# A four-layer graph network on one core: sums of three layers by scans, and row buffers released in quarters

## The chip, the cores and the metric

The kernel runs on 1 core of one Trainium2 chip, as a single program. The metric is the device time of one execution in microseconds (us), lower is better. Each row of a profile below is of one profiled execution. Engines: PE is TensorE, DVE is VectorE, ACT is ScalarE, POOL is GpSimd (it issues the gathers here), SP is SyncE (it issues the other loads and stores).

## What is computed

A graph has 6250 nodes with 64 features and 106250 edges (50000 pairs in both directions and a self-loop per node), sorted by destination. Four layers follow one another; each adds its result to x and normalizes:

```python
x = _layernorm(x + _L0_gnn_ref(x, L0_gnn_weight, src, dst, edge_type_16))        # sum over edges of x[src] @ W[type], 16 types
x = _layernorm(x + _L1_gnn_ref(x, L1_gnn_beta, src, dst))                        # softmax over a node's edges of the cosine of both ends
x = _layernorm(x + _L2_gnn_ref(x, edge_index, W_l, W_r, att, bias))              # GATv2 attention with 6 heads of 64
x = _layernorm(x + _L3_gnn_ref(x, W, coeff, h_bias, loop_weight, src, dst, edge_type_8))   # 2 bases, 8 types, plus x @ loop_weight
```

In each layer the core of the work is the same: a row of features per edge is fetched by the edge's source, weighted, and summed over the edges of one destination (`segment_sum`). The edges are in order of destination, so such a sum is a running sum that begins anew where the destination changes.

## The kernel before, in words

**Layout.** Edges lie over 128 partitions in NC = 832 columns; each partition holds a run of consecutive edges. Work goes in chunks of CH = 16 columns, NCH = 52 of them. `gf` holds one number per edge: 1 where the edge has the destination of the edge before it, 0 where a new one begins. The layers come one after another, and each has its loop over the 52 chunks.

**Gathers.** For each column POOL issues one indirect DMA that fetches 128 rows of a table in DRAM by the edges' sources (`gather`, L189, its instruction at L190), 16 per chunk. They go into a ring of buffers, and before a chunk's first gather POOL waits until the chunk that had the buffer is done with: in layer 0 (`linear_chunk_g`, L491, ring of N0 = 8) until the sums of it and of the first column after it are formed and stored; in layer 1 (`g1_chunk`, ring of 4) until the product of rows and weights (L838, L839) is made; in layer 2 (`g2_chunk`, L1165, ring of NX = 5) until all products of that chunk are made, DVE's (semaphore p2) and the 33 of ACT (semaphore ap, L1366 and L1371); in layer 3 (`basis_chunk_g`, L1640, ring of 4) until the product (L1663) is made. Layer 0's first FR = 5 chunks are made from the raw input and stand outside the change.

**Running sums.** DVE forms them column by column: SCALAR_TENSOR_TENSOR computes this column = previous column x gf + this column, on 64 (layer 0, L514), 65 (layer 1, L850), 390 (layer 2, L1385) or 128 elements (layer 3, L1673) per partition. Each instruction raises a semaphore and each waits for the one before it, as its input is that one's output. Layer 1 also spreads the destination's own row over its edges that way (`fill1`, L779, into PSUM; layer 2 does it at L1191). SP stores each chunk's sums in DRAM (s0 to s3). When a layer's last chunk is stored, POOL gathers the sum at each node's last edge from there ("s<-AR" is the store; "AR<-s,endi" the gather of ends), which starts the work per node.

**Beside the sums in layer 0** DVE prepares something else for the next layers. For 26 of its chunks two histograms run per chunk: DVE writes one-hots (L364, L366), PE multiplies them (L372, 16 small matmuls per histogram), and the next one-hots wait for that (semaphore hpe). After each chunk's histograms come two small operations of `twin_v` (L2052, L2055), then the 16 accumulations: `for c in range(FR, NCH): hists, twins, linear_chunk_v`.

**Layer 1** interleaves by hand, on DVE: the sums of chunk c (`step1`), the nine softmax steps of chunk c+1 (`soft1`, L800 to L820), the fill of c+2 (`fill1`); ACT makes the exponentials of c+1 (`exp1_a`, L828, L829) and DVE the product (`px1`, L838, L839).

**Layer 2** uses all engines: PE transposes the rows (L1205), multiplies with the weights (L1220, out by ACT at L1227), forms the logits with 32-column weights (L1236, out by ACT at L1244), and transposes these (L1251, out by ACT at L1256); DVE makes the softmax; products of weights and rows are made for some heads by DVE (L1354) and for two heads per column by ACT (L1371, `px2_a`); DVE sums (L1385).

**Layer 3**: a one-hot of the edge type (L1650), its product with the coefficients (L1652) and a reduction (L1655) give two weights per edge; L1663 multiplies rows and weights (2048 elements), then the 16 accumulations (L1673). In chunks 8 to 14 the self-loop's products are added: `turn3_a` (ACT copies a transposed block out of PSUM), PE at L1705, DVE at L1715 and L1717 (`loop3_v`). In ACT's queue the seven `turn3_a` stand right behind layer 2's work, with nothing else between.

## Time and profile before

| | us |
|---|---|
| median of 3 runs | 6202.34 (6194.47 to 6212.94) |
| the profiled execution | 6149.63 |
| its span, first to last instruction | 6147.8 |
| PE busy | 1595.5 |
| DVE busy | 2871.9 |
| ACT busy | 1115.1 |
| POOL busy | 3520.1 |

The profiled execution lies 52.7 us under the median. A busy time is the sum of an engine's instructions, register and semaphore work not counted. "Waits" of an engine are its idle time, by what ended it. In such lines "remote" stands where the profile shows no instruction that ended right then. The chain that ended last goes 39% through DVE and 3% through POOL.

### The profile page before, as it was taken

Reading aid. Unit: us, or ns where it says so; the run is one execution under the profiler, and the core shown is the slowest. Engines: PE = TensorE matmul, PEld = TensorE weight load, DVE = VectorE, ACT = ScalarE, POOL = GpSimd, SP = SyncE. Lnnn points to the kernel's source line nnn. Section 1 sums busy time; section 2 is a strip of 40 time slices with the busy share of each in tenths; the row PEclk is TensorE's granted clock in tenths of the full one; section 3 lists DMA queues with packets and bytes.
Section 4 is the critical chain, followed back from the end, with each engine's and each line's share of the span. In section 5 each row is a group of like instructions: output and inputs, shape, how many; then the busy total and the mean of one; then the engine's idle time right before and its main releaser. Section 6 shows DMA issues by size and latency. Waiting matters only on the chain.

```text
span 6147.8 us, 31588 instructions
## 1 busy us (share of the span) xinstructions
PE 1595.5 (26%) x6543; PEld 813.1 (13%) x6543; DVE 2871.9 (47%) x7562; ACT 1115.1 (18%) x3419; POOL 3520.1 (57%) x3636
## 2 busy tenths in 40 slices
PE   5531110000000000002375566666664500000002
PEld 1421110000000000001122222222221400000001
DVE  2344444125354455544255565555556632444344
ACT  1100000000000000001155555555555400000000
POOL 5355666766666666664634544454442576676754
PEclk7765555555555555556687888888887655555555
DMA  4212222221222222221123333333334221222222
GB/s 140 105 53 62 65 67 72 72 67 61 51 72 65 64 70 72 69 67 37 49 103 122 140 139 129 125 140 139 129 124 157 67 67 54 65 79 76 67 68 72
DMA packets 185944, 529.62 MB, mean 86 GB/s; under 512 B 70454, under 2 KB 75170, under 8 KB 169480
## 3 DMA queue, kind: packets, MB, share of 16 engines
q1 hardware_dynamic: 65816, 395.51, 17.0%
q0 software_dynamic: 117696, 129.81, 10.5%
q10 hardware_dynamic: 2224, 2.13, 0.1%
q14 instruction: 151, 1.24, 0.1%
q8 instruction: 57, 0.93, 0.1%
HBM read 185.57 MB, written 341.44 MB: 86 GB/s over the span
## 4 chain that ended last, share of the span: by engine, by line
DVE 39%; another core or an unknown queue 24%; issue 18%; PE 11%; ACT 5%; POOL 3%; DMA 1%; DVEq 0%; ACTq 0%; POOLq 0%; SPq 0%
DVE AR L1673 10%; DVE AR L514 5%; DVE ps L779 5%; PE ps L1220 4%; POOL AR L190 2%; PE ps L1236 2%; DVE AR L850 2%; DVE AR L1385 2%; ACT AR L1371 2%; DVE AR L364 1%; DVE AR L1663 1%; ACT AR L1227 1%; DVE AR L800 1%; PE ps L680 1%
## 5 line engine op out<-in xcount | busy, mean ns | idle before, releaser
L190 POOL DMA_INDIRECT AR<-xt,Si x2496 | 2402.0, 962 | 1687.3 <-issue 743.9
L190 POOL DMA_INDIRECT AR<-y,R x752 | 721.4, 959 | 520.9 <-issue 222.2
L1385 DVE SCALAR_TENSOR_TENSOR AR<-AR,gf 128x390 f32<-128x390 f32 x780 | 484.2, 621 | 654.3 <-ACT AR L1371 458.3
L1220 PE MATMUL ps<-AR,WLR 128*128 128x512 f32 x1248 | 681.7, 673 | 131.6 <-ACT AR L1227 88.2
L1673 DVE SCALAR_TENSOR_TENSOR AR<-AR,gf 128x128 f32<-128x128 f32 x831 | 295.0, 355 | 472.6 <-DVE AR L1673 360.1
L1371 ACT ACTIVATE AR<-AR 128x64 f32<-128x64 f32 x1664 | 495.5, 346 | 0.0
L1227 ACT ACTIVATE AR<-ps 128x512 f32<-128x512 f32 x624 | 368.5, 591 | 210.9 <-remote 146.7
L779 DVE SCALAR_TENSOR_TENSOR ps<-ps,gf,AR 128x64 f32<-128x64 f32 x831 | 242.2, 291 | 303.5 <-remote 160.5
L514 DVE SCALAR_TENSOR_TENSOR AR<-AR,gf 128x64 f32<-128x64 f32 x831 | 237.5, 286 | 258.2 <-DVE AR L514 155.5
L190 POOL DMA_INDIRECT AR<-s,endi x196 | 215.5, 1100 | 186.8 <-issue 112.4
L1220 PEld LDWEIGHTS ps<-AR,WLR 128*128 128x128 f32 x1248 | 238.8, 216 | 436.7 <-issue 312.5
L1354 DVE TENSOR_TENSOR AR<-AR,ps 128x512 f32<-128x512 f32 x416 | 282.8, 680 | 5.3 <-ACT ps L1329 5.3
L850 DVE SCALAR_TENSOR_TENSOR AR<-AR,gf 128x65 f32<-128x65 f32 x780 | 217.4, 279 | 100.7 <-remote 64.2
L1191 DVE SCALAR_TENSOR_TENSOR AR<-AR,gf 128x64 f32<-128x64 f32 x831 | 229.8, 277 | 48.4 <-DVE AR L1191 23.5
L364 DVE TENSOR_TENSOR AR<-AR,ps 128x1568 bf16<-128x1568 int32 x52 | 92.7, 1783 | 315.9 <-remote 291.4
L828 ACT ACTIVATE ps<-AR 128x17 f32<-128x17 f32 (+1 forms) x52 | 9.8, 188 | 1250.9 <-remote 431.8
L372 PE MATMUL ps<-AR 128*98 128x64 bf16 x832 | 80.1, 270 | 560.8 <-DVE AR L366 433.8
L1743 PE MATMUL ps<-ident,AR 128*128 128x128 f32 x1 | 0.5, 477 | 809.4 <-DVE AR L1673 809.4
L1992 ACT ACTIVATE AR<-AR 128x7 f32<-128x7 f32 x7 | 1.5, 208 | 1114.0 <-DVE AR L633 1067.9
L1236 PE MATMUL ps<-AR,A 128*32 128x512 f32 x1248 | 203.5, 604 | 0.0
L1016 PE MATMUL ps<-AR,ones 128*128 128x384 f32 (+1 forms) x6 | 3.7, 758 | 708.3 <-DVE AR L967 708.3
L1251 PE MATMUL ps<-ident,AR 128*128 128x128 f32 x208 | 55.3, 417 | 492.2 <-issue 319.1
(324 smaller groups left out, 2987.6 us busy)
## 6 DMA issues: line engine op xcount, KB each, us to landing
s<-AR SPq DMA_DIRECT2D x51, 3168.0 KB
AR<-xd SPq DMA_DIRECT2D x104, 512.0 KB
s<-AR SPq DMA_DIRECT2D x51, 1024.0 KB
AR<-xt,Si POOLq DMA_INDIRECT x2496
s<-AR SPq DMA_DIRECT2D x53, 512.0 KB
s<-AR SPq DMA_DIRECT2D x51, 528.0 KB
xd<-AR SPq DMA_DIRECT2D x52, 512.0 KB
y<-AR SPq DMA_DIRECT2D x24, 1024.0 KB
```

The source lines that it names most:

```text
L190: g.indirect_dma_start(out=o, out_offset=None, in_=table, in_offset=bass.IndirectOffsetOnAxis(ap=idx, axis=0)).then_inc(S[sem], 16)
L514: v.scalar_tensor_tensor(out=buf[:, j, :], in0=buf[:, j - 1, :] if j else prev[:, CH - 1, :], scalar=gf[:, c * CH + j:c * CH + j + 1], in1 ...
L779: v.scalar_tensor_tensor(out=xf1(c, j), in0=xf1(c, j - 1) if j else xf1(c - 1, CH - 1), scalar=gf[:, c * CH + j:c * CH + j + 1], in1=XBv[: ...
L850: v.scalar_tensor_tensor(out=Sv[:, j, 0:65], in0=Sv[:, j - 1, 0:65] if j else Sp[:, CH - 1, 0:65], scalar=gf[:, c * CH + j:c * CH + j + 1] ...
L1191: v.scalar_tensor_tensor(out=cur[:, j, D:P], in0=cur[:, j - 1, D:P] if j else prv[:, CH - 1, D:P], scalar=gf[:, c * CH + j:c * CH + j + 1] ...
L1220: t.matmul(PS[2 + k % 3][:], WLR[:, ch * P:(ch + 1) * P], XT2[:, u % 6, :], start=True, stop=True).then_inc(S["pm"], 1)
L1227: s.activation(RL2[:, u % 5, ch * 512:(ch + 1) * 512], PS[2 + k % 3][:], ACT.Relu).then_inc(S["ar"], 1)
L1236: m = t.matmul(PS[6][32 * q:32 * q + 32, :], w_, m_, start=(ch == 0), stop=(ch == 3))
L1354: v.tensor_tensor(s2v(c)[:, cols, 0:n * 65].rearrange("p j (h d) -> p j h d", h=n)[:, :, :, 0:D], bc(xsv(c)[:, cols, 0:D].unsqueeze(2), [P ...
L1371: s.activation(Sv[:, j, h * 65:h * 65 + D], xsv(c)[:, j, 0:D], ACT.Copy, scale=pe_[:, h, j:j + 1]).then_inc(S["ap"], 1)
L1385: m = v.scalar_tensor_tensor(out=Sv[:, j, 0:HW], in0=Sv[:, j - 1, 0:HW], scalar=gf[:, c * CH + j:c * CH + j + 1], in1=Sv[:, j, 0:HW], op0= ...
L1673: v.scalar_tensor_tensor(out=cur[:, j, :], in0=cur[:, j - 1, :] if j else prv[:, CH - 1, :], scalar=gf[:, c * CH + j:c * CH + j + 1], in1= ...
```

## The change

**Layers 0 (from chunk 5), 1 and 3.** The chain of 16 accumulations is replaced by scans. A `tensor_tensor_scan` computes, element after element along a partition, state = gate x state + data, here over 512 elements at a time. For this the data have to lie with the column as the fastest index, (d, j) in place of (j, d), and the gate has to be there for every element. So per chunk:

- ACT fills a PSUM bank with the gates (`gates_a`, 480 elements; the elements of column 0 stay at the 0 to which DVE's memset set the bank once: 4 banks ahead of layer 0's loop, 3 in layer 1, 3 + 1 in layer 3);
- in layer 0 ACT copies the gathered rows into a transposed tile (`turned0_a`), in layer 1 the destination's rows (`turned1_a`); the products of layers 1 and 3 are written transposed by DVE;
- DVE adds the previous chunk's last column in one instruction (semaphore st), then scans (semaphore sc): 2 of 512 elements in layer 0; 2 of 512 for the fill and 2 of 512 and one of 16 for the sums in layer 1; 4 of 512 in layer 3;
- ACT copies the sums out in store order (`summed0_a`, `summed1_a`, `summed3_a`: 1024, 1040, 2048 elements; semaphore co), and SP stores when co is raised, not when DVE is done.

POOL's releases: layer 0 now waits for the store alone (it ran that wait before too); layer 1 as before; layer 3 still for the product (m3). Layer 1's loads of destination rows wait for ACT's copy (cx).

**Order.** Layer 0's loop on DVE is now carry, twins, scans, then the two histograms. In layer 3 the three small weight operations of the next chunk stand between product, carry and scans of this one. The seven `turn3_a` now stand in ACT's queue in the middle of layer 3's loop (chunks 6 to 12), ahead of that chunk's copy out. Layer 1's last chunk is stored in halves instead of quarters, and the small `ends_v` of layer 1 moves from chunk 20 to chunk 49.

**Layer 2.** Its sums stay as they were. POOL's wait for the row buffer, once ahead of 16 gathers, becomes four waits, one ahead of each 4 gathers, for the products of the matching 4 columns.

```diff
@@ layer 0 @@
+        def gates_a(bank, at, n):
+            return s.copy(bank[:].rearrange("p (d j) -> p d j", j=n)[:, :, 1:n],
+                          bc(gf[:, at + 1:at + n].unsqueeze(1), [P, 512 // n, n - 1]))
...
+        def turned0_a(e, i):
+            c, j0, n = UN0[i]
+            e.wait_ge(S["late" if j0 else f"g_{c % N0}"], 16 * n if j0 else 16 * CH * (c // N0) + 16 * n)
+            if i >= 2:
+                e.wait_ge(S["st"], i)
+            s.copy(t0v(i), ring0(c)[:, j0:j0 + n, :].rearrange("p j d -> p d j")).then_inc(S["cx"], 1)
+
+        def summed0_a(e, i):
+            c, j0, n = UN0[i]
+            e.wait_ge(S["sc"], scans_upto(UN0, D, i + 1))
+            s.copy(ring0(c)[:, j0:j0 + n, :], t0v(i).rearrange("p d j -> p j d")).then_inc(S["co"], 1)
...
+            v.scalar_tensor_tensor(out=t0v(i)[:, :, 0], in0=row, scalar=gf[:, c * CH + j0:c * CH + j0 + 1],
+                                   in1=t0v(i)[:, :, 0], op0=ALU.mult, op1=ALU.add).then_inc(S["st"], 1)
...
+            for k in range(n * D // 512):
+                part = TT0[:, i % 2, k * 512:(k + 1) * 512]
+                v.tensor_tensor_scan(part, gx0(i)[:], part, 0.0, ALU.mult, ALU.add).then_inc(S["sc"], 1)
...
             if c >= N0:
                 e.wait_ge(S[f"s_{b}"], 16 * (c // N0))
-                e.wait_ge(S["lin0"], lin_at(c - N0 + 1, 0))
...
             for c in range(FR, NCH):
+                carry0_v(e, c - FR)
+                twin_v(e, 2 * (c - FR))
+                twin_v(e, 2 * (c - FR) + 1)
+                scan0_v(e, c - FR)
                 for h in hists(c):
                     hist_v(e, vc, 0, h)
-                twin_v(e, 2 * (c - FR))
-                twin_v(e, 2 * (c - FR) + 1)
...
-                linear_chunk_v(e, c)
@@ layer 1 @@
             for c in range(NCH):
-                exp1_a(e, c)
+                if c + 2 < NCH:
+                    gates1_a(e, c + 2)
+                    turned1_a(e, c + 2)
+                if c + 1 < NCH:
+                    exp1_a(e, c + 1)
+                summed1_a(e, c)
@@ layer 2 @@
         def g2_chunk(e, c):
-            if c >= NX:
-                e.wait_ge(S["p2"], p2_end(c - NX))
-                e.wait_ge(S["ap"], 33 * (c - NX + 1))
             for j in range(CH):
+                if c >= NX and j % 4 == 0:
+                    e.wait_ge(S["p2"], p2_end(c - NX) - 6 + j // 2)
+                    e.wait_ge(S["ap"], 33 * (c - NX) + 1 + 2 * (j + 4))
                 gather(xsv(c)[:, j, 0:D], xt2, Si[:, c * CH + j:c * CH + j + 1], f"g_{2 * (c % NX) + j // 8}")
@@ layer 3, on DVE, i a chunk or half of the last @@
+            v.tensor_tensor(sum3(i).rearrange("p (b d) j -> p j b d", b=NBS), bc(rows.unsqueeze(2), [P, n, NBS, D]),
+                            bc(CW3[:, i % 2, :, 0:n].rearrange("p b j -> p j b").unsqueeze(3), [P, n, NBS, D]),
+                            ALU.mult).then_inc(S["m3"], 1)
+            if more:
+                weight3_v(e, i + 1, 0)
...
+            for k in range(n * W3 // 512):
+                part = SUM3[:, i % 2, k * 512:(k + 1) * 512]
+                v.tensor_tensor_scan(part, gx3(i)[:], part, 0.0, ALU.mult, ALU.add).then_inc(S["sc"], 1)
+                if more and k == 0:
+                    weight3_v(e, i + 1, 2)
@@ layer 3, ACT's queue @@
-            for q in range(NG):
-                turn3_a(e, q)
+            gates3_a(e, 0)
+            for i, (c, j0, n) in enumerate(UN3):
+                if 6 <= c < 6 + NG:
+                    turn3_a(e, c - 6)
+                if i + 1 < len(UN3):
+                    gates3_a(e, i + 1)
+                summed3_a(e, i)
```

## Rows read from the trace of the kernel before

**Rows 1.** The page: busy time of each engine over the whole span.

```profile
PE 1595.5 (26%) x6543; PEld 813.1 (13%) x6543; DVE 2871.9 (47%) x7562; ACT 1115.1 (18%) x3419; POOL 3520.1 (57%) x3636
```

**Rows 2.** Busy time by stage; columns in the first line.

```profile
core 0: us, PE busy (x) PEld busy (x) DVE busy (x) ACT busy (x) POOL busy (x), PEclk, DMA share, GB/s
417.20:1041.60 624.40, 77.04 (x800) 70.42 (x800) 296.11 (x579) 0.00 (x0) 378.16 (x401) 0.50 0.22 63
1041.60:1351.00 309.40, 1.20 (x4) 1.00 (x4) 75.91 (x270) 0.00 (x0) 236.42 (x240) 0.50 0.26 77
1351.00:1406.60 55.60, 2.33 (x3) 1.17 (x4) 31.87 (x107) 0.00 (x0) 0.02 (x1) 0.50 0.31 124
1543.00:2764.20 1221.20, 1.46 (x4) 1.00 (x4) 594.78 (x2131) 16.23 (x100) 787.70 (x833) 0.50 0.26 67
2764.20:2804.20 40.00, 0.79 (x2) 0.50 (x2) 33.07 (x117) 0.65 (x4) 0.00 (x0) 0.50 0.14 55
2972.00:4631.50 1659.50, 1010.46 (x3763) 419.77 (x3756) 898.22 (x2300) 847.45 (x2602) 817.84 (x833) 0.81 0.36 125
4867.00:6030.20 1163.20, 30.19 (x122) 25.89 (x122) 450.71 (x1000) 3.85 (x13) 796.96 (x832) 0.50 0.23 67
6030.20:6064.70 34.50, 1.16 (x3) 0.68 (x3) 27.56 (x62) 0.27 (x1) 0.00 (x1) 0.50 0.26 104
```

**Rows 3.** POOL's longest waits for a buffer, layers 0 to 3: us, times, longest.

```profile
POOL AR L190 <- DVE AR L514: 140.2, 16, 15.1
...
POOL AR L190 <- DVE AR L839: 181.1, 16, 18.3
...
POOL AR L190 <- ACT AR L1371: 596.6, 47, 51.7
...
POOL AR L190 <- DVE AR L1663: 115.4, 15, 21.2
```

**Rows 4.** Timeline of layer 0 with histograms: start, duration, operation, [idle before].

```profile
584.76 1.54 PE L372 MATMUL ps<-AR 128*98 128x64 bf16 x16 [7.42 <-issue]
...
602.97 0.94 POOL L190 DMA_INDIRECT AR<-y,R  x1 [0.30 <-issue]
608.74 1.79 DVE L364 TENSOR_TENSOR AR<-AR,ps 128x1568 bf16<-128x1568 int32 x1 [24.04 <-remote]
...
613.73 0.94 POOL L190 DMA_INDIRECT AR<-y,R  x1 [9.81 <-DVE AR L514]
```

**Rows 5.** Timeline of layer 3, DVE, at two places.

```profile
5242.17 6.16 DVE L1673 SCALAR_TENSOR_TENSOR AR<-AR,gf 128x128 f32<-128x128 f32 x16
...
5690.99 2.29 DVE L1663 TENSOR_TENSOR AR<-AR,ps 128x2048 f32<-128x2048 f32 x1 [1.07 <-DVE ps L1655]
...
5702.79 0.35 DVE L1673 SCALAR_TENSOR_TENSOR AR<-AR,gf 128x128 f32<-128x128 f32 x1 [1.00 <-DVE AR L1673]
...
5718.99 2.29 DVE L1663 TENSOR_TENSOR AR<-AR,ps 128x2048 f32<-128x2048 f32 x1 [1.07 <-issue]
```

**Rows 6.** Timeline of layer 1, DVE's product of three chunks in a row.

```profile
1632.36 1.21 DVE L838 TENSOR_TENSOR AR<-AR,ps 128x1024 f32<-128x1024 f32 x1
...
1680.05 1.21 DVE L838 TENSOR_TENSOR AR<-AR,ps 128x1024 f32<-128x1024 f32 x1
...
1691.56 1.21 DVE L838 TENSOR_TENSOR AR<-AR,ps 128x1024 f32<-128x1024 f32 x1
```

**Rows 7.** Timeline of layer 2: PE's last logits, ACT's copy, POOL's next gather.

```profile
4389.65 1.04 PE L1236 MATMUL ps<-AR,Vm 128*32 128x512 f32 x8
...
4404.13 0.59 ACT L1244 COPY AR<-ps 128x512 f32<-128x512 f32 x1 [11.69 <-remote]
...
4416.26 0.99 POOL L190 DMA_INDIRECT AR<-xt,Si  x1 [14.66 <-ACT AR L1371]
```

**Rows 8.** Groups by line and shape: busy us, mean ns, idle before.

```profile
L1244 ACT COPY AR<-ps 128x512 f32<-128x512 f32 x52 | 30.5, 586 | 407.8 <-remote 373.0 <-issue 30.1 <-PE ps L1236 4.5
...
L1314 DVE TENSOR_TENSOR_SCAN AR<-AR 128x96 f32<-128x96 f32 x52 | 18.2, 350 | 0.0
...
L810 DVE TENSOR_TENSOR_SCAN AR<-Bn,AR 128x16 f32<-128x16 f32 x52 | 9.8, 189 | 18.1 <-remote 13.8 <-issue 2.2 <-DVE AR L807 2.0
```

More of the change, by code:

```diff
@@ L68, in stored_before @@
 def stored_before(L, b):
-    late = sum(m for l, (m, n) in enumerate(((16, N0), (48, 3), (48, 2))[0:L]) if b == (NCH - 1) % n)
+    late = sum(m for l, (m, n) in enumerate(((16, N0), (16, 3), (48, 2))[0:L]) if b == (NCH - 1) % n)
     return sum(16 * len(range(b, NCH, n)) for n in (N0, 3, 2, 3)[0:L] if b < n) + late
@@ L509, in linear_chunk_v @@
                     continue
-                if c == NCH - 1 and j == CH // 2:
-                    e.wait_ge(S["late"], 16 * CH // 2)
                 if c or j > 1:
@@ L1624, in build @@
         E8 = arena(6200, NC).bitcast(I32)
+        UN3 = [(c, 0, CH) for c in range(NCH - 1)] + [(NCH - 1, 0, CH // 2), (NCH - 1, CH // 2, CH // 2)]
+        W3 = NBS * D
+        SUM3 = arena(9100, 2, CH * W3)
         OH3 = PS[0][:, 64:64 + CH * R3].rearrange("p (j r) -> p j r", r=R3)
@@ L1677, in basis_chunk_y @@
-        def basis_chunk_y(e, c):
-            n = CH // 2 if c == NCH - 1 else CH
-            for j in range(0, CH, n):
-                e.wait_ge(S["lin3"], lin_at(c, j + n - 1))
-                load(e, columns_view(s3, c * CH + j, n), s3v(c)[:, j:j + n, :].rearrange("p j d -> p (j d)"), f"s_{c % 3}")
+            at = c * CH + j0
+            rows = GB[:, b, :].rearrange("p (j d) -> p j d", j=CH)[:, j0:j0 + n, :]
+            more = i + 1 < len(UN3)
+            if j0:
+                e.wait_ge(S["late"], 16 * CH + 16 * n)
+            else:
+                e.wait_ge(S[f"g_{b}"], gathered_before(3, b) + 16 * CH * (c // NBUF) + 16 * n)
@@ new lines, in basis_v @@
+            if i:
+                e.wait_ge(S["sc"], raised("sc", 3) + scans_upto(UN3, W3, i))
+                v.scalar_tensor_tensor(out=sum3(i)[:, :, 0], in0=sum3(i - 1)[:, :, UN3[i - 1][2] - 1],
+                                       scalar=gf[:, at:at + 1], in1=sum3(i)[:, :, 0],
+                                       op0=ALU.mult, op1=ALU.add).then_inc(S["st"], 1)
+            if more:
+                weight3_v(e, i + 1, 1)
+            if i:
+                e.wait_ge(S["st"], raised("st", 3) + i)
@@ L1989, in _ @@
                 raw_first_a(e, u)
+            gates0_a(e, 0)
+            for i in range(len(UN0)):
+                if i + 1 < len(UN0):
+                    gates0_a(e, i + 1)
+                turned0_a(e, i)
+                summed0_a(e, i)
             for q in range(NG):
@@ L2116, in _ @@
                 linear_chunk_v(e, c)
+            for bank in (2, 3, 4, 5):
+                v.memset(PS[bank][:], 0.0).then_inc(S["init"], 1)
             masks_v(e, vc, 0)
```

367 lines of the change are left out of this document (243 added, 124 removed), and 2 rows, old and new, of the table names.

## The prediction, made before the changed kernel was run

> **What bounds the kernel now.** I began with busy times [rows 1]: POOL leads with 3520 us of a span of 6148, 57%, so no engine is full and the time is somewhere in waits. The view by stage tells where [rows 2]. Nearly all of POOL's work is one instruction, a gather of 128 rows. Each takes 0.94 us and POOL needs 0.30 us more to issue the next (602.97 is the last of a stretch of them, each 1.25 us after the one before [rows 4]). A chunk has 16 gathers, so no layer can take less than 20.0 us per chunk. What the layers take, window over gathers times 16, is: layer 0 24.9 us while histograms run (624.4/401) and 20.6 after them (309.4/240), layer 1 23.5, layer 2 31.9, layer 3 22.4 [rows 2]. What lies above 20 is what POOL waits for a buffer to come free: 140, 181, 597 and 115 us [rows 3], in sum 1033. So the change can win at most these, and the stretches in which POOL stands idle behind the last gather of a layer: 55.6, 40.0 and 34.5 us [rows 2].
>
> Next question: why does the consumer fall behind, when DVE is busy for only 296 of 624, 595 of 1221, 898 of 1660 and 451 of 1163 us? The timelines answer it. In layer 3 the reader sees DVE multiply at 5690.99 and again at 5718.99: a chunk of 28.0 us with 20 instructions that each raise a semaphore, 1.4 us apart, where the next one starts 1.0 us after the end of the one before though it is the same engine. At 5242.17 the same 16 accumulations took 6.16 us, 0.385 each [rows 5]. I read this so: beside an unbroken row of gathers every completion that someone waits for is reported about a microsecond late. In layer 1 a chunk (43 such reports) took 47.7 us, 1.11 each, and the next one, with POOL just out of a pause, 11.5 us [rows 6].
>
> A second form is coarser. PE ends the histogram's products at 586.3 (584.76 + 1.54), and DVE, which waits for them, starts at 608.74, 24 us later and 4.8 us after POOL's last gather; POOL resumes at 613.73 [rows 4]. In layer 2 PE ends at 4390.7 and ACT starts its copy at 4404.13 after 11.7 us of idling; then POOL gets its whole row buffer at 4416.26, after 14.7 us of waiting [rows 7]. A report of PE seems to be held until POOL pauses. So POOL's rows of gathers slow the very work that it waits for.
>
> **The change, term by term.** Sums are made on the profiled execution, 6149.6 us; its span is 6147.8. It lies 52.7 us (0.8%) under the median, so the saving is set against the median in the end.
>
> *Scan duration.* Scans of 96 and 16 elements take 350 and 189 ns [rows 8]: (350-189)/80 = 2.0 ns per element, so 512 elements take 189 + 496 x 2.0 = 1.19 us. Bounds: 1.87 us by proportion to 96, and 0.57 us by the product's pace (2048 elements in 2.29 us [rows 5]). I take 1.19, the kind being the same.
>
> *Layer 0.* Sixteen accumulations become one carry and two scans: 16 x 0.28 (75.91/270 [rows 2]) = 4.5 us of DVE turn into 0.28 + 2.38 = 2.7, and 16 reports into 3. DVE's load matters little; the reports do. After the histograms the stage is at 20.6 already, 10 us to gain. With histograms the held report of PE stays (the two histograms per chunk stay), but the scan now lies ahead of them and the release of the buffer is no longer behind 16 slow accumulations: at 613.73 POOL still waited 5 us after DVE had woken [rows 4]. Some 2.4 us per chunk for 25 chunks: -60 for both parts. Bounds: -150 (all waits), +50 (27 us per chunk, if the wait moves to the next hold).
> Behind the last gather up to 16 late accumulations at 1.4 us and more still run; now half a chunk is one carry and one scan with two ACT copies, so 55.6 becomes some 11: -44.
>
> *Layer 1.* 43 reports (9 softmax, 2 products, 16 + 16 sums) become 18 (9, 2, 3 fills, 4 sums). Late ones at 1.11 to 1.4 us give 20 to 25 us per chunk, about the gathers' own pace, and only while POOL doesn't pause; quick chunks take under 11.5. So 23.5 becomes 21: 52 x 2.5 = -130. Bounds: 0 and -181. The stretch behind: 40 to 25, -15.
>
> *ACT's new work* in layers 0, 1 and 3: a gate copy of 480 elements at up to 0.59 us [rows 8] and copies of 1024 to 2048 elements, by the same row 1.2 to 2.4 us: at most 3 us per chunk on an engine that is busy 0 to 16 us in all of these stages [rows 2]. Costed at nothing, hidden by the 20 us of gathers with several chunks of ring between; without that cover it would be 3 us x 151 = 450 us. SP's stores start one copy later (1.2 to 2.4 us), against a ring of 3 or 8 chunks: nothing.
>
> *Layer 2.* Nothing of its work changes; only POOL's wait is cut in quarters of a chunk, 4 gathers or 5 us. Queued behind that wait are only further gathers; their readers are five chunks behind. POOL may start when ACT and DVE have done 4 columns of the old rows, and not 16. Own work per chunk is 19.4 us on PE, 17.3 on DVE, 16.3 on ACT (1010, 898, 847 over 52 [rows 2]); with a hold of 12 to 15 it makes 31.9. In [rows 7] 12.1 us pass from the end of the hold to the release. With quarters I expect the release after about a third of that, and a hold that lasts as before (once per chunk, until POOL has used up what was released): 31.9 - 8 + some 3.4 of holds that are now shorter but more frequent = 27.3 us, 52 x 4.6 = -240. Bounds: 0 (POOL starts sooner, and so the holds start sooner) and -597 (all waits).
>
> *Layer 3.* 20 reports become 9 (3 weights, product, carry, 4 scans). Late at 1.4 us they take 13 us, with 4 x 1.19 + 2.29 + 2 of own work under 16: below the 20 of the gathers. So the waits go but for the chunks with the self-loop's products, where ACT now waits for PE within its queue, and behind it stand the copies out that DVE's second buffer needs: -95 of the 115. Bounds: -123, and +50 (7 such chunks with 7 us more each). Behind the last gather 34.5 to 12: -22.
>
> *PSUM fills:* 11 memsets of 512 elements, each under a scan's length, partly hidden: +5.
>
> Sum: -60-44-130-15-240-95-22+5 = -601. From the median: 6202.3 - 601 = **5600 us**; on the profiled execution 5549.
>
> **A rule weighed.** Gathers take 0.943 us on average in the first part of layer 0 (378.16/401), 0.985 in its second part (236.42/240), where only accumulations run beside them, and 0.958 in layer 3 [rows 2]. If scans put that back to 0.943, it is 240 x 0.042 + 832 x 0.015 = 22 us more, and the time 5580; the sum above leaves it out, and it is inside the range. The Trainium skill ("SBUF — State Buffer", Who interferes with whom) states that a DVE instruction contends with GpSimd where it has two SBUF inputs, and not with one input in SBUF outside the two-port modes. By that rule, the accumulations would stretch gathers and scans with gates in PSUM would not.
>
> **Rivals.**
> *Forecast (A)*, 5480 to 5780: 0.55.
> *B, layer 2 nearly at the gathers' floor.* If pauses of POOL after each quarter let PE's reports through, no hold grows and layer 2 goes to 21 us per chunk: 327 us more, 5275. For: each engine's own work is under 20 us. Against: POOL at 20 us per chunk leaves no pauses, so the holds would come back. 0.14.
> *C, holds stay.* Layer 2 gains nothing and layer 0's histograms neither: 5600 + 240 + 60 = 5900. For: PE's reports are held by gathers, whose number is the same; starting POOL early lets it collide with the same work. 0.22.
> *D, slower.* Place: the new hand-overs between DVE and ACT in each scanned chunk (rows turned in, carry, scans, sums out, store). If ACT's waits are held as in [rows 7], a chunk costs what one in layer 2 does, 31.9: 15 x 11.3 + 52 x 8.4 + 52 x 9.5 = +1100 over 119 chunks, less 321 (layer 2 and the stretches behind), so about 6980. It decides the sign where the 119 chunks take 321/119 = 2.7 us more than their 22.7 of now, that is 25.4, one hold in about 2.2 chunks. For: ACT is put into a chain that was DVE's alone. Against: layer 1 has such a hand-over now (the exponential by ACT ahead of the product), and none of its three products shows idle time before it [rows 6]; only PE's reports show long holds. 0.06.
> *E, nothing moves* (POOL's pace or another holder sets it, so the waits change their names): 6200. 0.03.
>
> **How the numbers follow.** A, B and C are faster: 0.91. E splits to same 0.02 and slower 0.01; with D slower is 0.07. A measurement tells 0.3% apart, some 19 us. Low end 5270 takes in B; high end 5960 takes in C with its bounds in layer 3. Left out: D, E and the tails of A to C, 0.15 to 0.2.
>
> **What would show it.** Right, if: in layers 1 and 3 gathers run on at 1.25 us with POOL's waits for a release under 60 us in sum each; a scan takes 1.1 to 1.3 us; stretches behind the last gather are 10 to 25 us; layer 2 takes 26 to 29 us per chunk with ACT's copy behind PE's 32-column products still waiting some 5 to 8 us per chunk. Wrong, if: ACT's copies out or in start over 10 us after their scans or rows (D); layer 2 stays at 30 or more (C) or goes under 24 (B); a scan takes 1.8 us or more, which would make DVE's chunk of layer 3 some 3 us longer, still under 20.

## The result, and the profile after

The changed kernel takes **5817.3 us** (median of 4 runs, 5815.2 to 5821.6) beside 6198.4 us for the kernel before: ratio 0.938, interval 0.9365 to 0.940, 381 us less. It lies inside the range and 217 us above the number forecast. Later runs on other chips showed two quite different levels: 5718 us beside 6056 on one more (ratio 0.944, 0.942 to 0.947), and on two others 4807 to 4810 us for the kernel before, with variants of the changed one at 4812 to 4816. The experiments are about that too.

First the stages of the changed kernel by engine. The columns are those of [rows 2]. In order of the lines: layer 0's gathers, the gathers of its ends, layer 1's gathers and the stretch behind, layer 2's gathers, layer 3's gathers, the stretch behind, and the last stage.

```profile
193.40:1379.70 1186.30, 185.72 (x1320) 162.04 (x1320) 404.39 (x617) 228.31 (x222) 722.59 (x752) 0.54 0.23 67
1390.50:1543.60 153.10, 1.83 (x5) 0.57 (x3) 57.70 (x126) 2.92 (x14) 98.06 (x98) 0.52 0.12 32
1545.20:2709.00 1163.80, 0.00 (x0) 0.00 (x0) 531.51 (x935) 230.65 (x249) 790.73 (x832) 0.50 0.28 69
2709.00:2748.30 39.30, 2.94 (x8) 2.00 (x8) 32.50 (x70) 11.42 (x14) 0.00 (x1) 0.50 0.17 66
2918.10:4313.20 1395.10, 1015.34 (x3736) 424.24 (x3733) 893.30 (x2292) 849.39 (x2592) 846.19 (x832) 0.86 0.43 148
4554.00:5704.40 1150.40, 30.16 (x122) 25.89 (x122) 486.02 (x491) 215.90 (x119) 838.21 (x832) 0.50 0.24 71
5704.40:5715.60 11.20, 1.17 (x3) 0.69 (x3) 6.62 (x8) 2.19 (x2) 0.00 (x0) 0.50 0.13 50
5715.60:5814.10 98.50, 36.48 (x163) 28.76 (x163) 33.43 (x76) 9.99 (x23) 47.96 (x49) 0.60 0.17 49
```

Against [rows 2]: layer 1 went from 1221 to 1164 us, layer 2 from 1660 to 1395, layer 3 from 1163 to 1150. Layer 0's gathers end at 1379.7 and not at 1351.0, 29 us later; the stretch behind them fell from 55.6 to 10.8 us (1379.7 to 1390.5), but the gathers of its ends, 136 us before (1406.6 to 1543.0), took 153. Behind layer 3 34.5 fell to 11.2 us, and the last stage grew from 83.1 to 98.5. In sum the profiled execution lost 334 us of span (6147.8 to 5814.1), and layer 2 alone makes 264 of it. The medians differ by 47 us more; the profiled execution of before lay 49 us under its median, and no trace says what the other runs had in addition.

What the new instructions cost in layer 3 (groups by line and shape; L1855 are the scans, L1796 ACT's copies out, L1837 DVE's product):

```profile
L1855 DVE TENSOR_TENSOR_SCAN AR<-ps,AR 128x512 f32<-128x512 f32 x208 | 242.5, 1209 | 156.2 <-issue 91.6 <-ACT ps L515 64.6
L1796 ACT COPY AR<-AR 128x2048 f32<-128x2048 f32 x51 | 185.4, 3635 | 712.4 <-issue 473.8 <-DVE AR L1855 238.6
L1837 DVE TENSOR_TENSOR AR<-AR,ps 128x2048 f32<-128x2048 f32 x51 | 183.3, 3593 | 500.0 <-DMA AR<-xt,Si 500.0
```

A scan of 512 elements takes 1.21 us, where 1.19 was forecast. Turned accesses (those that read or write the data with rows and columns exchanged) cost more than forecast: ACT's copy of 2048 elements 3.6 us in place of at most 2.4, and DVE's product, now written turned, 3.6 in place of 2.29 [rows 5]. Neither is on the path: in layer 3 DVE's product now waits for its rows (500 us of idle time, "<-DMA AR<-xt,Si"), where before DVE ran behind. The scans did wait for ACT in the chunks with the self-loop: 156 us in five waits, for gates that stood in ACT's queue behind its waits of up to 45.8 us for PE.

POOL's waits, for layers 0 to 3 (us in total, times, longest), to be read beside [rows 3]:

```profile
POOL AR L191 <- DMA s<-AR: 154.8, 8, 21.2
...
POOL AR L191 <- remote: 124.6, 22, 7.0
...
POOL AR L191 <- DVE AR L1489: 233.5, 52, 37.7
POOL AR L191 <- ACT AR L1506: 85.5, 38, 4.0
...
POOL AR L191 <- DVE AR L1837: 41.4, 3, 24.4
```

Layer 0 waits 155 us where it waited 141 (from 417 us to its last gather), under another name: the store's, since that is now the last of its releases. Layer 1 went from 181 to 125 us, layer 2 from 597 to 319 (233.5 + 85.5), layer 3 from 115 to 41. But layer 3's saving of 74 us of waits gave 13 us of time. The gap is in the gathers: 838.21/832 = 1.007 us each in place of 0.958, and longer gaps between them, 61 us together.

These are means over stretches that differ a good deal. In the same layer, the windows run over chunks 1 to 8, the chunks with the self-loop and those that catch up behind them (10 to 19), chunks 20 to 28, and chunks 30 to 50:

```profile
4595.10:4756.20 161.10, 8.94 (x36) 7.58 (x36) 75.07 (x75) 29.29 (x17) 122.01 (x128) 0.50 0.25 72
4778.60:5031.10 252.50, 20.76 (x85) 17.81 (x85) 99.20 (x108) 48.21 (x31) 162.45 (x160) 0.50 0.23 68
5031.10:5212.30 181.20, 0.00 (x0) 0.00 (x0) 82.79 (x81) 36.75 (x18) 137.30 (x145) 0.50 0.27 78
5234.30:5683.20 448.90, 0.00 (x0) 0.00 (x0) 185.24 (x181) 81.65 (x40) 335.92 (x321) 0.50 0.24 70
```

So 17 chunks run at 20.1 us, the pace that the prediction called the floor. The chunks with the self-loop and those behind them take some 50 us more than that pace gives, and from chunk 30 on each takes 22.4 us. A chunk of that last stretch:

```profile
5305.89 1.21 DVE L1855 TENSOR_TENSOR_SCAN AR<-ps,AR 128x512 f32<-128x512 f32 x1
...
5307.33 3.44 DVE L1855 TENSOR_TENSOR_SCAN AR<-ps,AR 128x512 f32<-128x512 f32 x3
5308.34 1.24 POOL L191 DMA_INDIRECT AR<-xt,Si  x1 [0.63 <-issue]
...
5310.80 3.62 ACT L1796 COPY AR<-AR 128x2048 f32<-128x2048 f32 x1 [18.32 <-issue]
```

Products start at 5301.53 and 5323.96, 22.4 us apart, and not 20.0. None of DVE's reports is late here, although POOL gathers beside them: from the product's start to the last scan's end (5307.33 + 3.44) pass 9.2 us, all of it work.

Two more places. In layer 0 PE ends a histogram's products at 584.11 + 1.54 = 585.7, and DVE starts the next one-hots 27.9 us later; it is the hold of [rows 4], which was 22.4 us there (608.74 - 586.3). It ends here while POOL gathers on without a break:

```profile
584.11 1.54 PE L373 MATMUL ps<-AR 128*98 128x64 bf16 x16 [5.04 <-DVE AR L367]
...
612.34 0.95 POOL L191 DMA_INDIRECT AR<-y,R  x1 [0.31 <-issue]
613.56 1.79 DVE L365 TENSOR_TENSOR AR<-AR,ps 128x1568 bf16<-128x1568 int32 x1 [25.75 <-issue]
613.59 0.95 POOL L191 DMA_INDIRECT AR<-y,R  x1 [0.30 <-issue]
```

Of the 16 stretches of over 5 us in which DVE idles before such one-hots (417 to 1080 us), eight end with POOL stopped and eight while it gathers on; before the change 12 of 13 ended with POOL stopped. So a hold can end without a pause of POOL, which the prediction's reading of [rows 4] did not allow for.

In layer 2, to be read beside [rows 7], PE's report reaches ACT 1.9 us after POOL has stopped (3347.88 + 0.95), ACT has then waited 4.7 us in place of 11.7, and POOL goes on after 4.7 us in place of 14.7:

```profile
3347.88 0.95 POOL L191 DMA_INDIRECT AR<-xt,Si  x1 [0.30 <-issue]
3350.76 0.60 ACT L1362 ACTIVATE AR<-ps 128x512 f32<-128x512 f32 x1 [4.70 <-remote]
3351.74 0.57 ACT L1379 COPY AR<-ps 128x512 f32<-128x512 f32 x1
...
3353.54 1.16 POOL L191 DMA_INDIRECT AR<-xt,Si  x1 [4.71 <-DVE AR L1489]
```

The wait now stands before another of ACT's instructions: not before the copy of the 32-column products (L1244 before, L1379 now) but before the copies of the weight products (L1227 before, L1362 now). First before, then after, each the group's sums:

```profile
L1227 ACT ACTIVATE AR<-ps 128x512 f32<-128x512 f32 x624 | 368.5, 591 | 210.9 <-remote 146.7 <-PE ps L1220 50.1 <-issue 11.8
```

```profile
L1362 ACT ACTIVATE AR<-ps 128x512 f32<-128x512 f32 x624 | 368.7, 592 | 414.6 <-remote 234.6 <-PE ps L1355 126.6 <-issue 51.3
...
L1379 ACT COPY AR<-ps 128x512 f32<-128x512 f32 x52 | 30.0, 577 | 29.4 <-remote 24.7 <-PE ps L1371 4.6
```

With the 407.8 us of L1244 in [rows 8], both together fell from 619 to 444 us.

### The profile page after: what moved, and what is told of

Read it like the earlier page. It is cut to its first block, busy times and chain, and to the rows that moved or that the text cites. A ratio compares the mean times of both kernels' runs of the same rounds, so it can differ in the third digit from the quotient of the medians.

```text
span 5814.1 us, 30173 instructions
## 1 busy us (share of the span) xinstructions
PE 1605.1 (28%) x6543; PEld 817.4 (14%) x6543; DVE 2732.9 (47%) x5146; ACT 1758.2 (30%) x3826; POOL 3594.6 (62%) x3636
## 4 chain that ended last, share of the span: by engine, by line
PE 14%; POOL 13%; another core or an unknown queue 10%; issue 8%; ACT 5%; DVE 3%; DMA 0%; DVEq 0%; ACTq 0%; POOLq 0%
POOL AR L191 13%; PE ps L1355 8%; PE ps L1371 2%; ACT AR L1506 2%; ACT AR L1362 1%; PE ps L1340 1%; PE ps L1386 1%; DVE AR L1520 1%; PE ps L1219 0%; ACT AR L1379 0%; ACT AR L1347 0%; ACT AR L1796 0%; DVE AR L1855 0%; PE ps L1698 0%
## 5 line engine op out<-in xcount | busy, mean ns | idle before, releaser
L191 POOL DMA_INDIRECT AR<-xt,Si x2496 | 2475.2, 992 | 1284.4 <-issue 749.7
L1362 ACT ACTIVATE AR<-ps 128x512 f32<-128x512 f32 x624 | 368.7, 592 | 414.6 <-remote 234.6
L1837 DVE TENSOR_TENSOR AR<-AR,ps 128x2048 f32<-128x2048 f32 (+1 forms) x53 | 187.3, 3533 | 509.1 <-DMA AR<-xt,Si 509.1
L1796 ACT COPY AR<-AR 128x2048 f32<-128x2048 f32 (+1 forms) x53 | 189.4, 3574 | 725.3 <-issue 477.5
L1855 DVE TENSOR_TENSOR_SCAN AR<-ps,AR 128x512 f32<-128x512 f32 x208 | 242.5, 1209 | 156.2 <-issue 91.6
L535 ACT COPY AR<-AR 128x1024 f32<-128x1024 f32 (+1 forms) x48 | 90.0, 1876 | 647.3 <-DVE AR L555 505.9
L1326 DVE SCALAR_TENSOR_TENSOR AR<-AR,gf 128x64 f32<-128x64 f32 x831 | 230.1, 277 | 48.7 <-DVE AR L1326 26.6
L1924 PE MATMUL ps<-ident,AR 128*128 128x128 f32 x1 | 0.5, 477 | 742.6 <-DVE AR L1855 742.6
L857 ACT COPY AR<-AR 128x1040 f32<-128x1040 f32 (+1 forms) x53 | 102.6, 1938 | 200.2 <-remote 159.1
```

Source lines behind the costliest of these rows:

```text
L191: g.indirect_dma_start(out=o, out_offset=None, in_=table, in_offset=bass.IndirectOffsetOnAxis(ap=idx, axis=0)).then_inc(S[sem], 16)
L857: s.copy(Sv[:, j:j + n, 0:65], sum1(c)[:, :, j:j + n].rearrange("p d j -> p j d")).then_inc(S["co"], 1)
L1326: v.scalar_tensor_tensor(out=cur[:, j, D:P], in0=cur[:, j - 1, D:P] if j else prv[:, CH - 1, D:P], scalar=gf[:, c * CH + j:c * CH + j + 1] ...
L1362: s.activation(RL2[:, u % 5, ch * 512:(ch + 1) * 512], PS[2 + k % 3][:], ACT.Relu).then_inc(S["ar"], 1)
L1796: s.copy(s3v(c)[:, j0:j0 + n, :], sum3(i).rearrange("p x j -> p j x")).then_inc(S["co"], 1)
L1837: v.tensor_tensor(sum3(i).rearrange("p (b d) j -> p j b d", b=NBS), bc(rows.unsqueeze(2), [P, n, NBS, D]), bc(CW3[:, i % 2, :, 0:n].rearra ...
```

## The experiments

In what follows, "late reports" stands for what the prediction read from [rows 5] and [rows 7] (an instruction starts about 1 us, or many, after the end of the one that it waits for), and "prompt" for their absence.

**Theory.** The savings add up by stage; nearly all of it is the quarter release, which lets POOL stop early and often, so that PE's held reports come through. **Rivals.** The parts work on one another; the grain of the release is what is left; in layer 0 the holds of PE set the pace, not the sums; in layer 3 the scans or the turned copies stretch the gathers.

**1. Four variants together.** The edits: (e1) the kernel before with layer 2's quarter waits alone; (e2) the changed kernel with the whole-buffer wait put back,

```diff
             for j in range(CH):
-                if c >= NX and j % 4 == 0:
-                    e.wait_ge(S["p2"], p2_end(c - NX) - 6 + j // 2)
-                    e.wait_ge(S["ap"], 33 * (c - NX) + 1 + 2 * (j + 4))
```

with the two whole waits ahead of the loop again; (e3) the waits ahead of every 2 gathers,

```diff
-                if c >= NX and j % 4 == 0:
-                    e.wait_ge(S["p2"], p2_end(c - NX) - 6 + j // 2)
-                    e.wait_ge(S["ap"], 33 * (c - NX) + 1 + 2 * (j + 4))
+                if c >= NX and j % 2 == 0:
+                    e.wait_ge(S["p2"], p2_end(c - NX) - 7 + j // 2)
+                    e.wait_ge(S["ap"], 33 * (c - NX) + 1 + 2 * (j + 2))
```

and (e4) three buffers of one-hots in layer 0:

```diff
-                e.wait_ge(S[f"hpe{min(k, 1)}"], k // 2 * NCH + ch)
-            v.tensor_tensor(ohh, ...
+                if k or ch >= 3:
+                    e.wait_ge(S[f"hpe{min(k, 1)}"], k // 2 * NCH + (ch if k else ch - 2))
+            ring = 0 if k else ch % 3
+            v.tensor_tensor(OHH[ring], ...
```

> The kernel before with one edit: POOL's wait in layer 2 in quarters. The changed kernel's layer 2 took 1395.1 us from first to last gather, against 1658.9 before. Theory 1 (the quarter alone does this): layer 2 comes to 1390 to 1410 us, all other stages stay, the time is about 6200 - 264 = 5935, ratio 0.957. Rival (something else in the change, such as the state of the queues or where POOL enters the layer, has a part in it): over 1450 us in layer 2, ratio 0.965 or more.

> The changed kernel with the whole-buffer wait put back in layer 2: scans alone. Theory 1: 5817 + 264 = 6080, ratio 0.981; layer 1 stays at 1164 us for its gathers, layer 3 at 1150, layer 0 at 1186. Rival: the parts don't add up, the ratio is under 0.97 or over 0.99.

> The changed kernel with POOL's wait in layer 2 ahead of every 2 gathers in place of every 4. In the changed kernel layer 2 took 26.8 us per chunk, 16 gathers at a mean pace of 1.39 us (22.3) and 4.7 us of longer waits. Theory A (the grain of the release is what is left): 1.5 to 2.5 us per chunk less, layer 2 at 1270 to 1320 us, ratio 0.92 to 0.925. Theory B (what is left are reports of PE that come late while POOL gathers, and gathers stretched beside DVE; neither depends on the grain): layer 2 within 30 us of 1395, ratio 0.935 to 0.942.

> The changed kernel with three buffers of one-hots in layer 0, so that DVE waits for PE's products of three histograms ago and not of the one before. In the changed kernel DVE waited 291 us there without a releaser that the profile shows, 18 times, and 50 us passed per two chunks as before the change. Theory (PE's late reports set the pace of layer 0 while histograms run, and neither the scans nor their place ahead of the histograms touch that): DVE's waits there fall under 150 us, POOL's waits for stores of 155 us fall under 60, layer 0 is 60 to 130 us shorter, ratio 0.918 to 0.928. Rival (DVE's own work or the store of the sums sets the pace): layer 0 within 20 us of before, ratio 0.936 to 0.942.

Measured: none of this. The kernel before itself took 4809.8 us on this chip, and the four 4809.5, 4815.9, 4815.9 and 4812.1: ratios 0.9998 (0.9988 to 1.0007), 1.0013 (1.0003 to 1.0022), 1.0014 (1.0005 to 1.0024), 1.0004 (0.9994 to 1.0013). First to last gather of layers 1 to 3 of e1, then of layers 2 and 3 of e3:

```profile
1203.90:2246.90 1043.00, 1.46 (x4) 1.00 (x4) 585.94 (x2218) 16.56 (x102) 789.73 (x832) 0.50 0.32 79
2391.80:3477.60 1085.80, 943.84 (x3864) 375.13 (x3868) 929.41 (x2362) 878.22 (x2699) 832.42 (x832) 0.98 0.57 196
3678.00:4724.10 1046.10, 29.73 (x122) 25.45 (x121) 471.68 (x1049) 3.80 (x12) 792.80 (x832) 0.50 0.27 78
```

```profile
2394.20:3484.30 1090.10, 943.68 (x3864) 374.86 (x3868) 928.88 (x2361) 877.53 (x2699) 836.77 (x832) 0.97 0.57 196
3684.70:4730.20 1045.50, 30.16 (x122) 25.89 (x122) 486.11 (x491) 215.33 (x119) 792.15 (x832) 0.50 0.27 78
```

In both, scans or none, 832 gathers take 1043 to 1090 us, 1.25 to 1.31 us apiece, where the prediction called 1.25 the floor. Layer 3 of e1, still with its 16 accumulations, shows why:

```profile
4302.79 2.29 DVE L1663 TENSOR_TENSOR AR<-AR,ps 128x2048 f32<-128x2048 f32 x1 [10.49 <-DMA AR<-xt,Si]
...
4305.11 6.23 DVE L1673 SCALAR_TENSOR_TENSOR AR<-AR,gf 128x128 f32<-128x128 f32 x16
```

POOL gathers beside them without a break, and yet the 16 take 6.2 us and not the 22 of the slow chunks in [rows 5]. So gathers don't make reports late by themselves. The first trace of the kernel before, on a chip with late reports, has such chunks too, 55 accumulations in a row of them from 5388 to 5420 us:

```profile
5397.15 0.94 POOL L190 DMA_INDIRECT AR<-xt,Si  x1 [0.30 <-issue]
5397.80 6.16 DVE L1673 SCALAR_TENSOR_TENSOR AR<-AR,gf 128x128 f32<-128x128 f32 x16
5398.39 0.97 POOL L190 DMA_INDIRECT AR<-xt,Si  x1 [0.30 <-issue]
```

There the late reports come and go within a layer; in the set of this experiment none is seen. Where none is, DVE is done after 10 of 20 us, the gathers set the time, and the change has nothing to shorten.

**2. The changed kernel as it is, once more.**

> The changed kernel, unchanged, beside the kernel before. In the last four runs the kernel before took 4810 us, not 6198, and no edit moved it by over 0.2%: there POOL gathers at 1.25 us apiece through all four layers (1043, 1086 and 1046 us for the 832 of a layer) and next to nothing waits. Theory 1: reports to a waiting engine come late beside gathers in one condition of the chip and at once in another; where they come at once the change gives 4810 to 4820 us, ratio 1.000 to 1.003, where they come late 5817, ratio 0.938. Rival: the changed kernel as a whole does something that the four variants did not, and moves the time by over 0.5% where before takes 4810.

Another chip, and the late reports were back: 5718.5 us beside 6055.6, ratio 0.944 (0.942 to 0.947). That is neither of the two levels expected: the first chip's 0.938 lies outside the interval, and layer 2 took 56 us less than there. The changed kernel without any edit never met a chip with prompt reports, so for that case only its variants speak. The stages of this run serve for the comparisons that follow:

```profile
190.70:1363.80 1173.10, 189.14 (x1320) 164.37 (x1320) 404.94 (x617) 228.15 (x222) 722.24 (x752) 0.54 0.23 68
1528.30:2683.20 1154.90, 0.00 (x0) 0.00 (x0) 535.62 (x947) 230.54 (x249) 789.17 (x832) 0.50 0.28 70
2886.00:4225.20 1339.20, 1001.38 (x3733) 420.71 (x3733) 893.21 (x2292) 852.50 (x2593) 849.07 (x832) 0.87 0.45 155
4462.10:5609.80 1147.70, 30.16 (x122) 25.90 (x122) 485.94 (x491) 215.83 (x119) 833.61 (x832) 0.50 0.24 71
```

Kernels that ran together on one chip all met the same kind. Five of the seven sets met late reports, on at least three chips, and two met prompt ones, on two chips. What makes the difference was not found; nor is it shown that it is the chip itself and not a state that it was in, as, so far as is known, only one chip served two sets.

**3. Scans alone, three one-hot buffers, and layer 3 unturned.** The first two are the kernels e2 and e4 above, on a chip with late reports. The third:

```diff
-            s.copy(s3v(c)[:, j0:j0 + n, :], sum3(i).rearrange("p x j -> p j x")).then_inc(S["co"], 1)
+            s.copy(S3[:, c % 3, j0 * W3:(j0 + n) * W3], SUM3[:, i % 2, 0:n * W3]).then_inc(S["co"], 1)
...
-            v.tensor_tensor(sum3(i).rearrange("p (b d) j -> p j b d", b=NBS), ...
+            v.tensor_tensor(SUM3[:, i % 2, 0:n * W3].rearrange("p (j b d) -> p j b d", b=NBS, d=D), ...
```

> Scans alone once more (whole-buffer wait put back in layer 2), meant for a chip on which reports come late, as on the one where the kernel before took 6055 us and the changed one 5718. Theory 1 there (the quarters are worth what layer 2 lost, 264 us, and only layer 2 changes): ratio 0.944 + 264/6055 = 0.988, layer 2 back at 1600 to 1660 us. Rival (the parts work on one another): ratio under 0.975 or over 1.0. If before takes about 4810 us: 1.001 again.

> Three buffers of one-hots in layer 0 once more. Where before takes about 6055 to 6200 us: theory (PE's late reports set layer 0's pace while histograms run): its gathers take 1050 to 1120 us in place of 1173 to 1186, ratio 0.92 to 0.935. Rival (something else sets it): within 20 us, ratio 0.941 to 0.948. If before takes about 4810 us: 1.000 again.

> The changed kernel with layer 3's product written, and its sums copied out, without turning (the same elements in plain order, so that layer 3's sums are not those of the reference). Layer 3 gained 12 us where 95 were forecast: POOL's waits for a release fell from 115 to 41 us, but its gathers were stretched from a mean pace of 1.27 to 1.33 us, between 3 and 17 us after each product. DVE's turned product took 3.5 us in place of 2.3, ACT's turned copy 3.6. Theory S (turned accesses stretch the gathers): pace back under 1.28 us, layer 3 at 1100 us in place of 1150, ratio 0.008 lower. Rival (the scans, or stores of DVE's results, stretch them): pace stays at 1.31 or more and layer 3 stays within 20 us. If before takes about 4810 us: no stretch either way, within 0.2%.

The third kernel scans layer 3's data in plain order and so does not form the layer's sums. Before took 6046.8 us. **Scans alone:** 5983.3, ratio 0.9895 (0.987 to 0.992), close to theory 1's 0.988; layer 2 took 1597.7 us, just under its 1600 to 1660. Layer 2 is the one stage that moved against the changed kernel of run 2, by 1597.7 - 1339.2 = 258.5 us, and against the two other kernels on this chip, which have the quarters (1334.8 and 1332.9), by 263 to 265:

```profile
2888.10:4485.80 1597.70, 1038.46 (x3765) 424.09 (x3762) 899.87 (x2300) 845.31 (x2604) 814.94 (x832) 0.83 0.37 130
```

and POOL's wait for the whole buffer is there again, 46 times, as 47 times in [rows 3]:

```profile
POOL AR L191 <- ACT AR L1506: 526.8, 46, 51.4
```

So all the scans together are worth 1.05% (0.8 to 1.3), some 64 us, and the quarters, on top of the scans, the rest of the 5.6%. The quarters without the scans met only the chip with prompt reports, so that they would give the same alone is not shown.

**Three one-hot buffers:** 5693.0, ratio 0.9407 (0.938 to 0.943), by the interval no different from 0.944 for sure. Layer 0's gathers took 1143.1 us, where the two other kernels on the same chip took 1168.2 and 1169.7: 25 to 27 us less, where 60 to 130 were expected, and the rival's 20 is nearer. DVE's waits for PE while histograms run:

```profile
DVE AR L369 <- remote: 374.4, 14, 40.5
```

With one more wait of 6.2 us it is 381 us in 15 waits; the changed kernel of run 2 had 379 us in 32 (299.6, 60.0 and 19.6 by releaser), the longest 36.2. DVE waits less often but longer, and as long in sum, where under 150 us were expected. One reading is that a hold grows with the room that POOL has to go on; no run varied that room alone.

**Layer 3 unturned:** 5728.5, ratio 0.9476 (0.945 to 0.950). Theory S falls. ACT's copy fell from 3.6 to 1.9 us and the product to 2.3, and the layer took 1147.6 us as before, with gathers of 850.71/832 = 1.022 us:

```profile
4451.90:5599.50 1147.60, 30.17 (x122) 25.90 (x122) 419.74 (x491) 126.39 (x119) 850.71 (x832) 0.50 0.22 71
```

**4. Waits ahead of every 2 gathers, and layer 3 without scans.** The kernel e3 again, and

```diff
-                v.tensor_tensor_scan(part, gx3(i)[:], part, 0.0, ALU.mult, ALU.add).then_inc(S["sc"], 1)
+                v.tensor_tensor(part, part, gx3(i)[:], ALU.mult).then_inc(S["sc"], 1)
```

The second leaves out layer 3's running sums.

> POOL's wait in layer 2 ahead of every 2 gathers, meant for a chip with late reports. In the changed kernel's trace PE's report reaches ACT 1.7 to 1.9 us after POOL has stopped for a quarter, after 4.7 us of waiting by both; a chunk there takes 27.3 us. Theory A (a hold ends where POOL stops, and POOL stops sooner if it may go on for 2 gathers only): the pauses get shorter, layer 2's gathers take 1280 to 1320 us in place of 1335 to 1339 (or 1395 on the first chip), ratio 0.010 or more under that of the changed kernel there (0.944). Theory B (each stop costs the same whatever its grain, so more stops cost more or the same): within 20 us or slower, ratio 0.941 to 0.955. Where before takes about 4810 us: 1.001.

> The changed kernel with each of layer 3's scans replaced by a product of the same two inputs and the same size, so that the running sums of layer 3 are left out (0.57 us by the pace of its other product, not 1.2). Theory (the scans stretch layer 3's gathers, plain or turned access doesn't): mean pace of gathers from 1.33 to under 1.29 us, layer 3 at 1090 to 1110 us in place of 1148, ratio 0.007 to 0.009 less. Rival (ACT's copy or the store behind it stretches them): pace stays over 1.31, layer 3 within 15 us of 1148. Where before takes about 4810 us: 1.001.

Before took 6058.6 us. **Eighths:** 5721.5, ratio 0.944 (0.942 to 0.946), layer 2 in 1332.9 us: theory B. A chunk's long wait got shorter (3.4 us in place of 4.7, from the timeline of layer 2), and ACT still waits 4.9 us:

```profile
3161.03 0.59 ACT L1379 COPY AR<-ps 128x512 f32<-128x512 f32 x1 [4.92 <-remote]
...
3162.84 0.94 POOL L191 DMA_INDIRECT AR<-xt,Si  x1 [3.42 <-ACT AR L1506]
```

But there are more waits, 116 for ACT's products where the changed kernel of run 2 had 51:

```profile
POOL AR L191 <- ACT AR L1506: 200.0, 116, 35.6
```

The two other kernels of experiment 3 took 1333 and 1335 us in this layer with quarters. Quarters take what a finer release can.

**Layer 3 without scans:** 5725.8, ratio 0.9457 (0.944 to 0.948). DVE's 208 instructions took 0.68 us in place of 1.21, and the layer 1147.3 us:

```profile
4465.10:5612.40 1147.30, 30.16 (x122) 25.89 (x122) 379.12 (x491) 215.90 (x119) 841.77 (x832) 0.50 0.24 71
```

The scans don't stretch the gathers either. Three forms of layer 3 (run 2's, unturned, without scans) on three chips with late reports took 1147.3 to 1147.7 us, where two chips with prompt ones took 1045 to 1046 for the same gathers, with scans and without. In each of the three the 22.4 us per chunk begin at about chunk 30, as on the first chip, and the earlier chunks without a self-loop take 20.1. What stretches the later ones is open. It needs what makes reports late on these chips, but that is not enough: the kernel before, on the first chip, had gathers of 0.958 us in this layer. Of what the change brought in, the turned order and the scans are each ruled out alone; ACT's copy of every sum and the later store are not.

**5. A break behind each gather.** (e11) one fill of one element by POOL behind each gather of the four loops, (e12) two in layers 1 to 3:

```diff
+                g.memset(pad[32 * 1:32 * 1 + 1, c * CH + j:c * CH + j + 1], 0.0)
```

> The changed kernel with one small fill by POOL (1 element) behind each of the 3248 gathers of the four loops, so that no two gathers follow one another directly. Layers 1 and 3 take about 22.1 to 22.4 us per chunk (1.38 to 1.40 per gather) where reports come late, with or without scans or turned copies in layer 3, and 20.1 where they don't. Theory R (gathers in an unbroken row leave no room for other reports, and PE's get through only where POOL stops; a short break after each gather lets them through): where before takes about 6050 us, layer 2's gathers and layer 0's first part speed up, POOL's waits halve, and the time falls by 50 us or more under the changed kernel's 5720, ratio under 0.936. Rival (the break must be some microseconds long, or what delays reports is not the gathers' pace): the fills only add their own 0.05 to 0.15 us, the ratio is 0.944 to 0.98. Where before takes about 4810 us: gathers are the pace, so 3248 fills of 0.05 to 0.15 us add 160 to 490 us, ratio 1.03 to 1.10.

> The changed kernel with two small fills by POOL (1 element each, 0.10 us) behind each gather of layers 1, 2 and 3. One fill had hidden in the 0.30 us between two gathers, whose pace stayed 1.25 us; two should bring the pace to 1.35 to 1.40 us. Theory P (where reports come late, layers 1 and 3 can't go under 1.38 us per gather on average whatever POOL does, since what it gains in an unbroken row it gives back in stretches and waits): where before takes about 6050 us, layers 1 and 3 stay within 20 us of 1155 and 1148, while POOL's waits for a release and the stretches shrink, and layer 2 doesn't get slower than 1337 by more than 20; ratio 0.94 to 0.955. Rival (pace and waits are independent, so the fills add to both): 0.10 to 0.15 us x 832 = 80 to 125 us more in each of the three layers, ratio 0.985 or more. Where before takes about 4810 us the fills add 80 to 125 us per layer: ratio 1.05 to 1.08.

**One fill**, with late reports: 5726.5 beside 6052.2, ratio 0.9468 (0.9435 to 0.950). Where nothing else disturbs it the pace stays at 1.25 us from start to start, so the fill made no break, and it says nothing on theory R. Layers 1 to 3 took 1166, 1357 and 1163 us, 11 to 18 more than in run 2, of which layer 1's 11 lie within what runs of the same layer differ by (1146 to 1164):

```profile
5008.13 0.94 POOL L192 DMA_INDIRECT AR<-xt,Si  x1 [0.21 <-issue]
5009.07 0.10 POOL L1827 MEMSET pad<- 1x1 bf16 x1
...
5009.38 0.95 POOL L192 DMA_INDIRECT AR<-xt,Si  x1 [0.21 <-issue]
```

**Two fills** met a chip with prompt reports: 4814.7 beside 4807.0, ratio 1.0018 (1.0008 to 1.0027), layer 1 in 1038.3 us and not 80 to 125 more. What was expected for such a chip (80 to 125 us more per layer, ratio 1.05 to 1.08) fails: even two fills hide in the 0.30 us between gathers. Theory P was not put to the test, but the 17 chunks of layer 3 at 20.1 us, above, already speak against a floor of 1.38 us per gather. What pause a held report needs, if any, stays open.

## Why the prediction was right and where it was not

- **Layer 2, -240:** measured -264 on the first chip, and 263 to 265 between kernels with and without the quarters on another. POOL starts before the whole chunk is done, as described, and 31.9 us per chunk became 26.8 against 27.3. The place of the hold was not as forecast: ACT's copy behind the 32-column products was to wait 5 to 8 us per chunk and waits 0.6 (29.4/52), while the waits before the copies of the weight products doubled (211 to 415 us). In the sum the holds shrank from 619 to 444 us. So the size is right by a sum whose two parts, 8 us and 3.4 us, no run shows singly.
- **Layer 0, -60:** the gathers ended 29 us later. This step failed outright. It took 16 late accumulations for a part of the release; but DVE's work fell by 60 us over the same 624 us (296 to 236) and its waits for PE grew by 65 (314 to 379), so that PE's held reports set the cycle and the scans end early only to wait in it. Nor does the hold itself last 24 us in [rows 4], as the prediction has it, but 22.4; 24.0 is DVE's idle time. The stretch behind, -44, was right (-44.8), but 17 us of it went again in the gathers of ends, whose cause wasn't traced.
- **Layer 1, -130:** measured -57. The size of a late report was the error. The forecast had 18 at 1.11 to 1.4 us, 20 to 25 us per late chunk; a late chunk takes 26.7 (exponentials at 2099.82 and 2126.47), 1.48 each, so DVE stays behind POOL. The 1.11 to 1.4 us held the short accumulations' own work; DVE's own 10.2 us per chunk (531.5/52) and 18 times the 0.84 to 0.97 us by which a report was late before give 25 to 28. Behind the layer nothing was gained (39.3 against 40.0) where 15 were forecast.
- **Layer 3, -95:** measured -13. POOL's waits went from 115 to 41 us, where 20 were to be left; the rest is the gathers and their gaps, 61 us longer than before, a term that the forecast put at nothing. It took 20.0 us per chunk as the pace once the waits are gone, and 17 chunks had 20.1; but from chunk 30 on it was 22.4. The self-loop's chunks and those behind them cost some 50 us over that pace, as much as the forecast's bound of +50: ACT stood up to 45.8 us for PE there, and DVE for ACT's gates. The sum for DVE's chunk was wrong too: 9 reports that are 1.0 us late and 9 us of own work make 18 us and not "under 16". It did no harm, as DVE's reports came promptly in this layer and its work took 9.2 us. The stretch behind, -22, was right (-23).
- **ACT's work at nothing:** right but for the self-loop's chunks, though its turned copies took half as long again as the highest price given. Rival D had the hand-overs to ACT held like PE's; they weren't. In layer 3 ACT's copy starts 0.03 us after the last scan's end (5310.80 against 5307.33 + 3.44). D's "one hold in about 2.2 chunks" does not follow from its own figures: 2.7 us of the 9.2 by which 31.9 exceeds 22.7 are one in 3.4.
- **The rule weighed:** its 22 us did not come. From before to after, on the first chip, gathers went from 0.985 to 0.967 us in the second part of layer 0 (239.79/248), from 0.945 to 0.950 in layer 1 and from 0.958 to 1.007 in layer 3. With prompt reports they take 0.95 us in layer 3 beside accumulations and beside scans (792.80 and 792.15 over 832). The Trainium skill's statement on two SBUF inputs ("SBUF — State Buffer", Who interferes with whom), which it makes of a GpSimd instruction that reads SBUF, is neither borne out nor refuted by that; the reading of [rows 2] that led to the 22 us was wrong.
- **The signs given:** the scan's 1.21 us, 26.8 us per chunk in layer 2, layer 3's 41 us of waits and the stretches of 10.8 and 11.2 us came as said. Layer 1's 125 us of waits (under 60), its stretch of 39.3 us (10 to 25), gathers at 1.25 us all through layer 3, and ACT's 5 to 8 us (0.6) did not.
- **Which case came:** between A (to 5780) and C (5900): layer 2 as in A, layer 0 as in C. The gathers of layers 0, 1 and 3 together gave 41 us where 285 were forecast, so the total is in the range by the range's width and by layer 2, the largest term. What no case had was that late reports come on some chips and not on others. The range held for the chip on which it was measured, by 143 us; on the two prompt ones variants of the change show an effect of none to +0.2%.

## What to carry to other kernels

Where a producer stops for a buffer and its consumer waits for reports that come late while the producer runs, try to release the buffer in parts: a wait per quarter was worth 4% here, and halving it again nothing. Before a chain of dependent instructions is rewritten as scans, ask whether the chain or a hold elsewhere in the same loop sets the pace; here all of it was worth 1%. Look at a layer's pace chunk by chunk before calling its mean a floor. And run a kernel whose waits end in "remote" on a second chip before explaining them: the same program took 4810 us on one and 6198 on another.
